# A two-layer graph network on one core: the middle part reordered, second-layer sums in three products

## The chip, the core and the metric

The kernel runs on one core of one Trainium2 chip. A core has five engines with queues of their own: TensorE (PE in the profile), VectorE (DVE), ScalarE (ACT), GpSimd (POOL) and SyncE (SP), which here issues most of the loads. They meet only through semaphores. The metric is the device time of one execution in microseconds (us), as the median over runs.

## The reference, cut to what matters

There are 625 nodes of 512 features and 10,000 edges. Layer 0 is a gated graph convolution of two steps beside a linear-attention block and a small feed-forward; layer 1 is a graph convolution with attention (`_L1_gnn_ref`) beside a second linear attention (`_L1_mix_ref`), and then two experts. The changed places are these:

```python
# layer 0, second graph step; A[r] are the 625 x 625 gated adjacencies of the two edge types
w = einsum('rb,bio->rio', att, basis)                 # 30 bases, summed per type
out = sum_r (A[r] @ (gate_r * h)) @ w[r] + h @ root + bias
# layer 1, convolution over neighbours
xb = batchnorm(xn);  agg = mean_over_neighbours(xb)   # agg = An @ xb
conv_out = relu(agg @ W_conv + b_conv)
h_attn = performer_attention(first 128 nodes) @ Wo    # later nodes repeat the last row
gnn = batchnorm(conv_out + h_attn + xn)
# layer 1, linear attention, all nodes, 8 heads of 64
q, k, v = xn @ w_qkv.T;  phi(t) = elu(t) + 1
kv = phi(k).T @ v * scale;  mix = (phi(q) @ kv) @ w_proj.T + b_proj
x = x + gnn + mix
```

## The kernel before, in words

The order of work on every engine is written out by hand: one function per engine (`block.sync`, `block.gpsimd`, `block.scalar`, `block.vector`, `block.tensor`), whose statements are that engine's queue. Nodes are handled as 5 row tiles of 125 or, with features on the partitions, as 4 feature blocks of 128 by two token halves of 312 and 313 (`HALF`). Matrices lie in eight `slot`s, whose names `row(s)` and `col(s)` say which of the two layouts is meant; `half[s]` are the same bytes under another type.

PE writes into 8 PSUM banks in a fixed rotation. `PSUM_ORDER` lists the stages and the number of tiles of each; `claim` makes PE wait until the tile eight places earlier has been read by ACT (`act_read`) or by DVE (a semaphore ending in `_out` or `_low`). So the order of stages also sets who must have finished before a bank comes free.

There are two kinds of product. A plain float32 product shows as two matmul records. The other kind splits both factors into a high and a low part of type fp32r and adds three products, high by high, high by low and low by high (`split_cols_out`, `split_rows_out`); each of these is one record. ACT, DVE or POOL makes the parts: a copy to the high part, a subtraction for the low part.

The stages in question, with the names of the code, are in order on PE:

- `o2`: `h1 @ root` (line 1456), then for both edge types r the product of the neighbour sums `Z` with the summed bases `wrel[1][r]` (line 1462), 40 plain products of 512 columns; DVE adds each row tile to x and normalises it.
- router and small feed-forward of layer 0 (lines 1472 to 1503), not touched.
- `aq`, `ak`, `av`: the three projections of the first 128 nodes. `xbr`: 20 transposes (line 1274) of the batch-normalised features to rows. `agg`: 40 plain products with the adjacency `An`, split by ACT and DVE as they come. `ad`, `uk`: squares and key features of the 128 nodes. `conv`: `agg @ W_conv`, 96 split products. `uq`, `kv`, `qfT`: the rest of the small attention's factors.
- `xqa` (half of the query projection), `at`, `atT` (line 1584), `ha` (the small attention's end), `xqb`, `xv`, `xk`, then `xkv` (phi(k).T @ v), `xo` (phi(q) @ kv), `xp` (the projection). phi is a chain of DVE (line 1134), ACT (line 755) and DVE (line 1143) per tile.
- DVE adds the convolution, `xn` and `ha` in three large steps (lines 1148 to 1152) between the first and second half of the queries, splits `xo` (line 1168), runs the second batch norm (lines 873 to 883) and adds `xp` (line 1175). `x3r`: 20 transposes back to rows, which DVE adds to x and normalises by tile (lines 1182, 861, 856); then `xeT` and the expert logits `el`.

POOL makes the split parts of the four linear weights (`split_linear`, lines 506 and 508) in two buffers that SP fills; `W_conv` is split by POOL in the same way.

## Time and profile before

| | before |
|---|---|
| median of 3 runs | 887.9 us (885.4 to 890.91) |
| the profiled execution | 887.52 us, of which 885.8 us are the span of the profile |
| mean granted TensorE clock | 0.957 |
| busy: PE, PEld, DVE, ACT, POOL | 830.7, 657.0, 527.6, 235.4, 148.8 us |
| chain that ended last | PE 87%, DVE 8%, ACT 2%, issue 2% |
| HBM read | 105.81 MB, 121 GB/s over the span |

PE is busy in 94% of the span and carries the chain. Its busy time counts records that overlap, so the length of a stage is taken here from the start of its first record to the start of the next stage. The rest of the chain (DVE, ACT, issue) is time in which PE waits for a factor that another engine prepares.

### The profile page before, as it was taken

What the parts mean: (1) busy time and instruction counts of PE and PEld (TensorE: products, weight loads), DVE (VectorE), ACT (ScalarE), POOL (GpSimd) and SP (SyncE); (2) the same over time, 40 slices, a digit from 0 to 9 for tenths busy, and PEclk for the clock granted to TensorE, in tenths of its full rate; (3) what the DMA queues carried; (4) which work ended last, traced back from release to release, by engine and by line L of the source; (5) the groups of instructions that cost most, each with busy time, mean ns of one, the idle gap of its engine ahead of it and who ended that gap; (6) DMA issues with size and microseconds to landing.
All of it is one profiled execution on the core that took longest, in us unless ns stands there. A gap on an engine that the chain in (4) does not pass through costs nothing.

```text
span 885.8 us, 10938 instructions
## 1 busy us (share of the span) xinstructions
PE 830.7 (94%) x4071; PEld 657.0 (74%) x4071; DVE 527.6 (60%) x746; ACT 235.4 (27%) x450; POOL 148.8 (17%) x96
## 2 busy tenths in 40 slices
PE   2999999998999999999998998989769999999997
PEld 1998758856667777764466698868758889998886
DVE  6877999936969999982267142946562211422112
ACT  3052223115411012220044242132342331323310
POOL 2010010021010000001000502600223431244210
PEclk9999998796999999999999998999769999999999
DMA  7732789984598768731040301000053121131101
GB/s 247 221 48 40 236 244 359 302 203 65 186 248 268 232 226 274 237 122 49 1 152 13 131 1 49 1 0 1 1 173 113 62 82 48 56 133 53 42 0 58
DMA packets 64211, 110.21 MB, mean 124 GB/s; under 512 B 6815, under 2 KB 16412, under 8 KB 64172
## 3 DMA queue, kind: packets, MB, share of 16 engines
q1 hardware_dynamic: 54476, 96.71, 32.9%
q0 software_dynamic: 6912, 7.70, 5.7%
q10 hardware_dynamic: 2784, 5.27, 1.6%
q8 instruction: 25, 0.41, 0.2%
q14 instruction: 14, 0.11, 0.0%
HBM read 105.81 MB, written 1.28 MB: 121 GB/s over the span
## 4 chain that ended last, share of the span: by engine, by line
PE 87%; DVE 8%; ACT 2%; issue 2%; DMA 1%; POOL 0%; DVEq 0%; SPq 0%; POOLq 0%
PE bank L1258 53%; PE bank L1655 13%; PE bank L1339 6%; PE bank L1462 4%; PE bank L1445 4%; PE bank L1456 2%; PE bank L1439 2%; DVE slot L1152 1%; PE bank L1267 1%; DMA slot<-in_x 1%; DVE st L861 1%; DVE slot L856 1%; ACT slot L570 1%; PE bank L1472 1%; PE bank L1274 0%
## 5 line engine op out<-in xcount | busy, mean ns | idle before, releaser
L974 DVE SCALAR_TENSOR_TENSOR weights<-weights,att 128x2048 f32<-128x2048 f32 x116 | 263.3, 2344 | 3.3 <-DMA weights<-in_L_gnn_basis 2.7
L1258 PE MATMUL bank<-half,ew_hi 128*128 128x312 f32 (+1 forms) x576 | 127.3, 310 | 2.2 <-POOL ew_lo L539 2.2
L1239 DVE CAST hid_hi<-slot 128x626 fp32r<-128x626 f32 x32 | 17.8, 557 | 159.8 <-ACT slot L817 159.8
L1258 PE MATMUL bank<-AT,slot 125*128 125x312 f32 (+1 forms) x400 | 105.9, 426 | 1.8 <-ACT slot L682 0.9
L1258 PEld LDWEIGHTS bank<-half,ew_hi 128*128 128x128 f32 x576 | 98.4, 191 | 5.9 <-issue 3.2
L1258 PEld LDWEIGHTS bank<-AT,slot 125*128 125x128 f32 x400 | 75.5, 189 | 31.8 <-ACT slot L682 1.1
L539 POOL TENSOR_TENSOR ew_lo<-weights,ew_hi 128x1024 fp32r<-128x1024 f32 x28 | 69.0, 2486 | 134.0 <-ACT ew_hi L799 134.0
L1258 PE MATMUL bank<-weights,slot 128*125 128x512 f32 (+5 forms) x306 | 90.5, 460 | 0.3 <-ACT slot L570 0.3
L1258 PE MATMUL bank<-half,ew_lo 128*128 128x312 f32 (+1 forms) x288 | 89.0, 309 | 0.0
L570 ACT ACTIVATE slot<-bank 128x312 f32<-128x312 f32 (+6 forms) x88 | 43.5, 526 | 146.9 <-PE bank L1258 107.8
L1258 PEld LDWEIGHTS bank<-weights,slot 128*125 128x125 f32 (+2 forms) x306 | 55.0, 214 | 30.2 <-issue 26.7
L817 ACT ACTIVATE slot<-bank,eb_now 128x312 f32<-128x312 f32 x64 | 33.3, 522 | 156.3 <-PE bank L1258 156.3
L1258 PE MATMUL bank<-slot,weights 128*128 128x313 f32 (+2 forms) x304 | 68.3, 386 | 0.8 <-ACT slot L570 0.8
L1258 PEld LDWEIGHTS bank<-slot,weights 128*128 128x128 f32 x304 | 51.1, 194 | 17.0 <-issue 1.5
L1655 PE MATMUL bank<-ew_lo,hid_hi 128*125 128x512 f32 x160 | 63.3, 396 | 0.0
L1655 PE MATMUL bank<-ew_hi,hid_lo 128*125 128x512 f32 x160 | 63.1, 395 | 0.0
L1655 PE MATMUL bank<-ew_hi,hid_hi 128*125 128x512 f32 x160 | 63.0, 394 | 0.0
L1339 PE MATMUL bank<-slot 125*125 125x312 f16 (+1 forms) x384 | 55.2, 306 | 1.2 <-DVE slot L959 1.1
L1339 PEld LDWEIGHTS bank<-slot 125*125 125x125 f16 x384 | 53.0, 141 | 3.1 <-DVE slot L959 1.9
L1258 PEld LDWEIGHTS bank<-half,ew_lo 128*128 128x128 f32 x288 | 55.2, 192 | 0.0
L958 DVE TENSOR_SCALAR slot<-slot,small 125x625 f16<-125x625 f16 x96 | 39.2, 408 | 13.9 <-issue 4.6
L570 ACT ACTIVATE slot<-bank,cols 128x312 f32<-128x312 f32 (+1 forms) x42 | 21.8, 526 | 87.6 <-PE bank L1445 46.4
(275 smaller groups left out, 1095.1 us busy)
## 6 DMA issues: line engine op xcount, KB each, us to landing
weights<-in_L_gnn_basis SPq DMA_DIRECT2D x60, 1024.0 KB, 5.5
weights<-in_L_ffn_W SPq DMA_DIRECT2D x32, 512.0 KB, 4.4
weights<-in_L_mix_kqv_w SPq DMA_DIRECT2D x1, 3072.0 KB, 10.3
weights<-in_w_qkvT SPq DMA_DIRECT2D x3, 1024.0 KB, 5.4
slot<-slot POOLq DMA_DIRECT2D x10, 250.0 KB, 5.2
weights<-in_L_mix_mlp_w ACTq DMA_DIRECT2D x2, 1024.0 KB, 16.4
weights<-in_L_gnn_root ACTq DMA_DIRECT2D x2, 1024.0 KB, 7.8
slot<-in_row_mlp_b POOLq DMA_DIRECT2D x1, 1250.0 KB, 34.0
```

What stands on the lines that cost most here:

```text
L539: pool.tensor_tensor(ew_lo[:, c % 4, at:at + 1024], weights[:, 2048 * (c % 2) + at:2048 * (c % 2) + at + 1024], ew_hi[:, c % 4, at:at + 10 ...
L570: act.activation(dst, src, func, **kw).then_inc(S("act_read"), 1)
L817: act.activation(hid[:, f % 4, a:a + w], B("eh", n % 3)[:, 0:w], ACT.Silu, bias=eb1_now[:, f:f + 1]).then_inc(S("eh_out"), 1)
L958: dve.tensor_scalar(oh_src[j % 2][u], iota_src, small[0:P, bass.ds(EU * q0 + EU * i + u, 1)], None, ALU.is_equal)
L974: ins = dve.scalar_tensor_tensor(wrel[layer][r], wmat(at), att[:, layer, r, b:b + 1], wrel[layer][r], ALU.mult, ALU.add)
L1239: dve.tensor_copy(hid_hi[:, f % 4, :], hid[:, f % 4, :]).then_inc(S("hid_high"), 1)
L1258: ins = pe.matmul(out, a, b, start=i == 0, stop=i == len(pairs) - 1)
L1339: ins = pe.matmul(bkq[0:P, 0:w], oh_dst[j % 2][u][:, P * r:P * r + P], oh_src[j % 2][u][:, a:a + w], start=False, stop=False)
L1439: pe.matmul(bk[:, 0:w], root[0][:, k, 128 * m:128 * m + 128], xnT[:, k, a:a + w], start=k == 0, stop=False)
L1445: ins = pe.matmul(B("h1T", n)[:, 0:w], wrel[0][r][:, k, 128 * m:128 * m + 128], col(Z_AT[r])[:, k, a:a + w], start=False, stop=i == 2 * KT ...
L1462: ins = pe.matmul(B("o2", j)[0:P, :], col(Z_AT[r])[:, k, P * j:P * j + P], wrel[1][r][:, k, :], start=False, stop=r == 1 and k == KT - 1)
L1655: ins = pe.matmul(B("eb2", j)[0:P, :], a, b, start=f == 0 and i == 0, stop=f == 15 and i == 2)
```

## The change

The function of every stage and the reference's values stay; what changes is this.

1. `o2`: the 40 plain products with `wrel[1]` become 120 split products. ACT makes the high parts (two of `Z`, two of the weights), DVE the low parts, after the last base has been summed.
2. The convolution's weight goes ahead of the neighbours: `xbw = xb @ W_conv` as 60 split products by rows, then `conv` as 40 plain products of `xbw` with `An`. The transposes `xbr` and the split of `agg` go; the split is now of `xb`, which comes with its bias from DVE's batch norm. `uk` and `ad` stand before `xbw`. POOL splits `W_conv` before the squares, and SP loads it earlier.
3. Keys and values (`xk`, `xv`) go ahead of the queries; `xkv` lies between `atT` and `ha`; `xq` is one stage of eight tiles, and `xq`, `xo` and `xp` go by token halves (`by_half`). DVE adds `xn` between the key tiles and `ha` between the query tiles, feature block by feature block.
4. `xp` and `x3r` become one stage `xpr` of 13 tiles: the first two row tiles are transposed after the fifth and the sixth tile of the projection, and DVE takes up the rows in that order.

On PE, the start of the middle part before (`weights 128x128` are `aq` and `ak`, line 1274 is `xbr`, `AT` is the adjacency, `half` the split `agg`):

```order
L1258 MATMUL bank<-slot,weights 128x128 x32
L1258 MATMUL bank<-weights,slot 128x512 x4
L1274 MATMUL bank<-ident,slot 125x128 x20
L1258 MATMUL bank<-AT,slot 128x312 x5
...
L1258 MATMUL bank<-halfsum,slot 128x2 x8
L1258 MATMUL bank<-weights,slot 128x256 x8
L1258 MATMUL bank<-half,ew_hi 128x312 x2
L1258 MATMUL bank<-half,ew_lo 128x312
...
L1258 MATMUL bank<-slot 128x65 x16
```

And the same place now (`ew_lo,half` are the split products `xbw`):

```order
L1291 MATMUL bank<-slot,weights 128x128 x32
L1291 MATMUL bank<-weights,slot 128x512 x4
L1291 MATMUL bank<-weights,slot 128x256 x8
L1291 MATMUL bank<-halfsum,slot 128x2 x8
L1291 MATMUL bank<-ew_lo,half 125x512 x60
...
L1291 MATMUL bank<-AT,slot 128x312 x5
L1291 MATMUL bank<-AT,slot 128x313 x5
...
L1291 MATMUL bank<-slot 128x65 x16
```

The 20 transposes are gone, the adjacency's products stand behind the weight's, and no 312-column split product is left in this part.

On DVE, from the first query tiles to the second batch norm, now (`bank,tmp` ends phi, lines 1188 and 1189 add `ha`, line 1197 splits `xo`):

```order
L1149 TENSOR_SCALAR tmp<-bank 128x312 [waits xq_out,psum_full]
L1188 TENSOR_TENSOR slot<-slot 128x128 [waits res,act_read]
L1189 TENSOR_SCALAR slot<-slot 128x497
L1159 SCALAR_TENSOR_TENSOR slot<-bank,tmp 128x312 [waits xexp]
L1149 TENSOR_SCALAR tmp<-bank 128x313 [waits xq_out,psum_full]
...
L1197 TENSOR_TENSOR hid_lo<-bank,hid_hi 128x312 [waits act_read,dve_step]
...
L885 BN_STATS tmp<-slot 128x6 [waits res]
```

Before, the additions were one block ahead of the last four query tiles:

```order
L1148 TENSOR_TENSOR slot<-slot 128x4x625 [waits act_read]
L1150 TENSOR_TENSOR slot<-slot 128x4x128 [waits act_read,dve_step]
L1152 TENSOR_SCALAR slot<-slot 128x497 x4
L1154 MEMSET slot 128x512 [waits dve_step]
L1134 TENSOR_SCALAR tmp<-bank 128x312 [waits xq_out,psum_full]
```

The four feature blocks are now added one at a time, each ahead of the step that ends a query tile's phi.

The diff, cut to its core:

```diff
-              ("xn2A", 12), ("aq", 1), ("ak", 1), ("av", 1), ("xbr", 5), ("agg", 8),
-              ("ad", 1), ("uk", 4), ("conv", 8), ("uq", 4), ("kv", 3), ("qfT", 4),
-              ("xqa", 4), ("at", 2), ("atT", 1), ("ha", 1),
-              ("xqb", 4), ("xv", 5), ("xk", 5), ("xkv", 1), ("xo", 8), ("xp", 8), ("x3r", 5),
+              ("xn2A", 12), ("aq", 1), ("ak", 1), ("av", 1), ("uk", 4), ("ad", 1), ("xbw", 5), ("uq", 4), ("conv", 8),
+              ("kv", 3), ("qfT", 4), ("xk", 5), ("at", 2), ("xv", 5), ("atT", 1), ("xkv", 1), ("ha", 1),
+              ("xq", 8), ("xo", 8), ("xpr", 13),
...
+def by_half(n):
+
+    return n % 4, HALF[n // 4]
...
+        z2_hi, z2_lo = (half[2], half[3]), (half[5], half[6])
+        w2_hi = [t.rearrange("p (k n) -> p k n", k=KT) for t in (ew_hi[:, 1, :], ew_lo[:, 0, :])]
+        w2_lo = [ew_hi[:, 2 + r, :].rearrange("p (k n) -> p k n", k=KT) for r in range(2)]
...
+        xb_hi, xb_lo = half[5], half[3]
+        conv_hi, conv_lo = (ew_lo[:, b, :].rearrange("p (k n) -> p k n", k=KT) for b in (1, 2))
...
+        xbw, xk_row, xv_row, xq, res = row(6), row(6), row(3), col(4), col(5)
...
+            load(W_conv, I["L1_gnn_W_conv"].rearrange("(k p) n -> p k n", p=128), "Wconv_in")
             load(Wq, I["L1_gnn_Wq"].rearrange("(k p) n -> p k n", p=128), "Wqkvo_in")
+            sp.wait_ge(S("psum_full"), filled("o2", 5))
             load(Wk, I["L1_gnn_Wk"].rearrange("(k p) n -> p k n", p=128), "Wqkvo_in")
-            sp.wait_ge(S("psum_full"), filled("o2", 5))
...
-            load(W_conv, I["L1_gnn_W_conv"].rearrange("(k p) n -> p k n", p=128), "Wconv_in")
...
+            sp.wait_ge(S("conv_split"), 1)
...
+            pool.wait_ge(S("Wconv_in"), 16)
+            pool.wait_ge(S("o2_low"), 4)
+            pool.tensor_copy(conv_hi, W_conv).then_inc(S("conv_high"), 1)
+            pool.wait_ge(S("conv_high"), 1)
+            pool.tensor_tensor(conv_lo, W_conv, conv_hi.bitcast(f32), ALU.subtract).then_inc(S("conv_split"), 1)
             pool.wait_ge(S("act_read"), READ0["ak"] + 1)
...
-            split_linear(0, filled("av", 1))
             pool.wait_ge(S("kmax"), 1)
             pool.partition_all_reduce(amax_kr, amax_k, 128, bass.bass_isa.ReduceOp.max).then_inc(S("kmax_all"), 1)
-            split_linear(1, filled("conv", 8))
-            split_linear(2, filled("ha", 1))
-            split_linear(3, filled("uq", 4))
+            pool.wait_ge(S("xb_low"), 4)
+            split_linear(0, filled("av", 1))
+            split_linear(1, filled("xbw", 5))
+            split_linear(2, filled("uq", 4))
+            split_linear(3, filled("ha", 1))
...
+                    if l == 1 and n % 8 == 7:
+                        act.wait_ge(S("act_read"), READ0["Z2"] + n + 1)
+                        act.activation(z2_hi[r][:, :, 0:N], col(Z_AT[r])[:, :, 0:N], ACT.Copy).then_inc(S("o2_high"), 1)
+            for r in range(2):
+                act.wait_ge(S("w_sum"), SUM_AT[1, NB - 1, r])
+                act.activation(w2_hi[r], wrel[1][r], ACT.Copy).then_inc(S("o2_high"), 1)
...
+            for r in range(2):
+                dve.wait_ge(S("o2_high"), r + 1)
+                dve.tensor_tensor(z2_lo[r][:, :, 0:N], col(Z_AT[r])[:, :, 0:N], z2_hi[r][:, :, 0:N].bitcast(f32),
+                                  ALU.subtract).then_inc(S("o2_low"), 1)
+                dve.wait_ge(S("o2_high"), r + 3)
+                dve.tensor_tensor(w2_lo[r], wrel[1][r], w2_hi[r].bitcast(f32), ALU.subtract).then_inc(S("o2_low"), 1)
...
+                dve.wait_ge(S("xb_high"), k + 1)
+                dve.tensor_tensor(xb_lo[:, k, 0:N], col(3)[:, k, 0:N], xb_hi[:, k, 0:N].bitcast(f32), ALU.subtract).then_inc(S("xb_low"), 1)
...
+            def add_xn2(n):
+                if n < KT:
+                    dve.wait_ge(S("act_read"), READ0["conv"] + 8)
+                    dve.tensor_tensor(res[:, n, 0:N], res[:, n, 0:N], col(2)[:, n, 0:N], ALU.add).then_inc(S("res"), 1)
+
+            phi(0, TT, add_xn2)
...
-            dve.wait_ge(S("act_read"), READ0["conv"] + 8)
-            link(dve.tensor_tensor(col(6)[:, :, 0:N], col(6)[:, :, 0:N], col(2)[:, :, 0:N], ALU.add))
-            dve.wait_ge(S("act_read"), READ0["ha"] + 1)
-            dve.tensor_tensor(col(6)[:, :, 0:NA], col(6)[:, :, 0:NA], haT, ALU.add)
-            for k in range(KT):
-                ins = dve.tensor_scalar(col(6)[:, k, NA:N], col(6)[:, k, NA:N], haT[:, k, NA - 1:NA], None, ALU.add)
-            link(ins)
...
+                if 0 <= k < KT:
+                    dve.wait_ge(S("act_read"), READ0["ha"] + 1)
+                    dve.wait_ge(S("res"), 4)
+                    dve.tensor_tensor(res[:, k, 0:NA], res[:, k, 0:NA], haT[:, k, :], ALU.add)
+                    dve.tensor_scalar(res[:, k, NA:N], res[:, k, NA:N], haT[:, k, NA - 1:NA], None, ALU.add).then_inc(S("res"), 1)
+
+            phi(TT, TT + 8, add_ha)
...
+            batchnorm(res, res, "g2", "bn2")
             dve.wait_ge(S("bn2"), 4)
...
+            def xp_tile(n):
+                m, (a, w) = by_half(n)
+                dve.wait_ge(S("psum_full"), filled("xpr", XP_TILE[n] + 1))
+                dve.scalar_tensor_tensor(res[:, m, a:a + w], B("xpr", XP_TILE[n])[:, 0:w], bsum[:, m:m + 1], res[:, m, a:a + w],
+                                         ALU.add, ALU.add).then_inc(S("xp_out"), 1)
+
             def x3_row(j):
-                dve.wait_ge(S("psum_full"), filled("x3r", j + 1))
-                dve.tensor_tensor(x[:, j, :], B("x3r", j)[0:P, :], x[:, j, :], ALU.add).then_inc(S("x3r_out"), 1)
+                for n in ((0, 1, 2, 3, 4), (5,), (6, 7), (), ())[j]:
+                    xp_tile(n)
+                dve.wait_ge(S("psum_full"), filled("xpr", X3_TILE[j] + 1))
+                dve.tensor_tensor(x[:, j, :], B("xpr", X3_TILE[j])[0:P, :], x[:, j, :], ALU.add).then_inc(S("x3r_out"), 1)
...
+            def split_cols(out, wh, wl, th, tl, m, a):
+                w = 314 if a else 312
+                return group(out[:, 0:w], [(wt[:, k, 128 * m:128 * m + 128], t[:, k, a:a + w]) for k in range(KT)
+                                           for wt, t in ((wh, th), (wh, tl), (wl, th))])
...
-                pe.wait_ge(S("w_sum"), SUM_AT[1, NB - 1, r])
+                pe.wait_ge(S("o2_low"), 2 * r + 2)
                 for j in range(TT):
                     for k in range(KT):
-                        ins = pe.matmul(B("o2", j)[0:P, :], col(Z_AT[r])[:, k, P * j:P * j + P], wrel[1][r][:, k, :],
-                                        start=False, stop=r == 1 and k == KT - 1)
+                        for i, (t, wt) in enumerate(((z2_hi, w2_hi), (z2_hi, w2_lo), (z2_lo, w2_hi))):
+                            ins = pe.matmul(B("o2", j)[0:P, :], t[r][:, k, P * j:P * j + P], wt[r][:, k, :],
+                                            start=False, stop=r == 1 and k == KT - 1 and i == 2)
                     if r == 1:
...
-            pe.wait_ge(S("xbT"), 4)
-            to_rows("xbr", col(3))
-            pe.wait_ge(S("act_read"), READ0["xbr"] + 5)
-            pe.wait_ge(S("act_read"), READ0["xn2A"] + 12)
...
+            bk = claim(pe, "ad")
...
+            pe.wait_ge(S("xb_low"), 4)
             pe.wait_ge(S("conv_split"), 1)
-            split_cols_out("conv", conv_hi, conv_lo, agg_hi, agg_lo)
+            for j in range(TT):
+                bk = claim(pe, "xbw", j)
+                group(bk[0:P, :], [(t[:, k, P * j:P * j + P], wt[:, k, :]) for k in range(KT)
+                                   for t, wt in ((xb_hi, conv_hi), (xb_hi, conv_lo), (xb_lo, conv_hi))]).then_inc(S("psum_full"), 1)
...
+            pe.wait_ge(S("act_read"), READ0["xbw"] + 5)
+            for n in range(8):
+                m, (a, w) = n // 2, HALF[n % 2]
+                bk = claim(pe, "conv", n)
+                group(bk[:, 0:w], [(xbw[:, i, 128 * m:128 * m + 128], An[:, i, a:a + w]) for i in range(TT)]).then_inc(S("psum_full"), 1)
...
-            split_cols_out("xqa", lin(ew_hi, "q"), lin(ew_lo, "q"), hid_hi, hid_lo, range(4))
+            split_rows_out("xk", "k")
...
+            pe.wait_ge(S("lin_split"), 2)
+            split_rows_out("xv", "v")
             bk = claim(pe, "atT")
...
+            bk = claim(pe, "xkv")
+            pe.wait_ge(S("xk_out"), 5)
+            pe.wait_ge(S("act_read"), READ0["xv"] + 5)
+            for p in range(KT):
+                ins = group(bk[:, 128 * p:128 * p + 128], [(xk_row[:, j, 128 * p:128 * p + 128], xv_row[:, j, 128 * p:128 * p + 128]) for j in range(TT)])
...
             pe.wait_ge(S("lin_split"), 3)
...
+            for n in range(8):
+                m, (a, w) = by_half(n)
+                split_cols(claim(pe, "xq", n), lin(ew_hi, "q"), lin(ew_lo, "q"), hid_hi, hid_lo, m, a).then_inc(S("psum_full"), 1)
...
+                m, (a, w) = by_half(n)
                 bk = claim(pe, "xo", n)
-                group(bk[:, 0:w], [(kvb[:, m, :], col(3)[:, m, a:a + w])]).then_inc(S("psum_full"), 1)
-            pe.wait_ge(S("xo_low"), 8)
+                pe.wait_ge(S("xq_out"), n + 1)
+                group(bk[:, 0:w], [(kvb[:, m, :], xq[:, m, a:a + w])]).then_inc(S("psum_full"), 1)
...
+            def projected(n):
+                m, (a, w) = by_half(n)
+                bk = claim(pe, "xpr", XP_TILE[n])
+                pe.wait_ge(S("xo_low"), 4 * (n // 4) + 4)
+                split_cols(bk, lin(ew_hi, "proj"), lin(ew_lo, "proj"), hid_hi, hid_lo, m, a).then_inc(S("psum_full"), 1)
+
+            def sum_row(j):
+                bk = claim(pe, "xpr", X3_TILE[j])
+                pe.wait_ge(S("xp_out"), 4 if j < 2 else 8)
+                for k in range(KT):
+                    ins = pe.transpose(bk[0:P, 128 * k:128 * k + 128], res[:, k, P * j:P * j + P], ident[:, :])
+                ins.then_inc(S("psum_full"), 1)
+
+            for n in range(8):
+                projected(n)
+                if n in (4, 5):
+                    sum_row(n - 4)
+            for j in range(2, TT):
+                sum_row(j)
```

## Rows read from the trace of the kernel before

**Rows 1.** Windows: length, busy time of each engine, PEclk (granted clock), DMA share, GB/s.

```profile
413.80:448.20 34.40, 34.40 (x82) 15.03 (x81) 7.45 (x16) 0.59 (x2) 0.00 (x0) 1.00 0.00 0
488.00:624.22 136.22, 126.53 (x728) 110.73 (x728) 63.34 (x101) 37.77 (x79) 36.10 (x15) 0.96 0.08 27
512.50:516.30 3.80, 3.80 (x33) 3.38 (x32) 1.35 (x3) 1.90 (x3) 0.00 (x0) 1.00 0.00 0
541.94:543.64 1.70, 1.70 (x8) 1.70 (x7) 0.00 (x0) 0.72 (x2) 1.70 (x1) 0.50 0.00 0
541.94:549.80 7.86, 7.86 (x51) 7.86 (x50) 0.00 (x0) 0.72 (x2) 2.77 (x1) 0.88 0.38 133
559.47:566.45 6.98, 6.98 (x51) 6.98 (x50) 6.95 (x3) 0.60 (x1) 6.52 (x2) 1.00 0.01 2
566.45:580.40 13.95, 13.56 (x60) 10.55 (x59) 13.09 (x12) 2.00 (x5) 8.90 (x3) 1.00 0.01 1
597.37:603.70 6.33, 6.33 (x40) 6.14 (x40) 0.00 (x0) 0.00 (x0) 0.00 (x0) 0.73 0.01 3
629.32:642.95 13.63, 11.44 (x60) 11.12 (x60) 7.72 (x18) 7.16 (x14) 6.30 (x5) 0.62 0.00 1
```

**Rows 2.** PE's timeline: start, length, instruction, [idle before it <- releaser].

```profile
477.19 7.31 PE L1258 MATMUL bank<-slot,weights 128*128 128x128 f32 x64
...
488.01 2.45 PE L1274 MATMUL bank<-ident,slot 128*125 128x128 f32 x20
...
491.35 21.30 PE L1258 MATMUL bank<-AT,slot 125*128 125x312 f32 x80 [0.90 <-ACT slot L570]
...
532.42 3.79 PE L1258 MATMUL bank<-slot 128*128 128x65 f32 x32
...
538.61 3.68 PE L1567 MATMUL bank<-ident,slot 128*128 128x128 f32 x16 [2.40 <-DVE slot L1112]
...
554.49 0.63 PE L1584 MATMUL bank<-ident,slot 128*128 128x128 f32 x4 [1.02 <-DVE slot L1119]
...
555.90 3.81 PE L1258 MATMUL bank<-slot,weights 128*128 128x128 f32 x32 [0.78 <-ACT slot L570]
...
597.37 6.33 PE L1258 MATMUL bank<-slot 125*128 125x128 f32 x40 [2.22 <-issue]
...
604.65 4.48 PE L1258 MATMUL bank<-slot 128*128 128x312 f32 x16 [0.95 <-DVE slot L1162]
...
610.17 0.41 PE L1258 MATMUL bank<-hid_hi,ew_hi 128*128 128x312 f32 x1 [1.04 <-DVE hid_lo L1168]
...
624.88 2.45 PE L1274 MATMUL bank<-ident,slot 128*125 128x128 f32 x20 [0.64 <-DVE slot L1175]
```

**Rows 3.** DVE's timeline, same columns.

```profile
393.98 0.41 DVE L1001 CAST b_split<-slot 1x512 fp32r<-1x512 f32 x1
...
524.66 2.76 DVE L1104 TENSOR_TENSOR hid_lo<-slot,hid_hi 128x2500 fp32r<-128x2500 f32 x1
...
564.10 12.00 DVE L1152 TENSOR_SCALAR slot<-slot 128x497 f32<-128x497 f32 x4
...
610.03 3.17 DVE L873 BATCH_NORM_STATS2 tmp<-slot 128x6 f32<-128x312 f32 x8
...
617.39 2.34 DVE L1175 SCALAR_TENSOR_TENSOR slot<-bank,small,slot 128x312 f32<-128x312 f32 x5
...
629.32 0.68 DVE L1182 TENSOR_TENSOR slot<-bank,slot 125x512 f32<-125x512 f32 x1
```

**Rows 4.** Line 1152 alone: nanoseconds least, median, most; first and last start.

```profile
L1152 DVE TENSOR_SCALAR slot<-slot x4: 465/3464/4841, 564.1 to 575.6; 128x497 f32<-128x497 f32 x4
```

**Rows 5.** POOL's timeline, columns as in rows 2.

```profile
396.87 5.72 POOL L487 TENSOR_TENSOR AT<-AT 125x3125 f32<-125x3125 f32 x1 [143.24 <-PE bank L1258]
...
563.71 4.94 POOL L508 TENSOR_TENSOR ew_lo<-weights,ew_hi 128x2048 fp32r<-128x2048 f32 x1
```

**Rows 6.** Groups of instructions, ACT: busy us, mean ns, idle before.

```profile
L613 ACT ACTIVATE slot<-slot 128x2500 f32<-128x2500 f32 x1 | 2.3, 2279 | 0.0
```

More of the change, by code:

```diff
@@ L735, in _ @@
                 act.activation(ke[:, h, :], ub("uk", h), ACT.Exp, bias=abias_k[:, h:h + 1]).then_inc(S("act_read"), 1)
-            for n in range(8):
-                m, (a, w) = n // 2, HALF[n % 2]
-                copy_out("conv", n, col(6)[:, m, a:a + w], B("conv", n)[:, 0:w], ACT.Relu, bias=colvec("b_conv", m))
+            for j in range(TT):
+                copy_out("xbw", j, xbw[:, j, :], B("xbw", j)[0:P, :])
             act.wait_ge(S("qbias"), 1)
@@ L867, in _, with batchnorm @@
             bns = [0]
-            def batchnorm(src, dst, gain, name):
+            def batchnorm(src, dst, gain, name, bias=None):
                 for k in range(KT):
```

187 lines of the change are left out of this document (75 added, 112 removed), and 4 rows, old and new, of the table ACT_READS.

## The prediction

> **What bounds the kernel now.** I read the page for the chain that ended last, then PE's timeline from the second layer's sums to the experts, then windows over the same stretch for the granted clock, then DVE's and POOL's timelines beside it. The order matters: the chain says that PE decides, the timeline says where PE waits, the windows say at which of its two levels (1.2 or 2.4 GHz) it works there.
>
> Three things are to be seen. First, `o2` with `wrel[1]` is 34.4 us of unbroken PE work at full clock [rows 1]. Second, from the end of `av` (488.00) to the last product of `xp` (624.22) there are 136.22 us, in which PE is busy for 126.53 [rows 1]; the waits are short and many: 0.90 before the adjacency, 2.40 before `qfT`, 1.02 and 0.78 around `atT`, 2.22 before `xkv`, 0.95 and 1.04 around `xo` [rows 2]. Third, some waits are paid twice, because the granted clock falls behind them: the first 1.70 us of `xqa`, behind the 2.40, run at 0.50, and `xkv`, behind the 2.22, at a mean of 0.73 [rows 1]. After `xp`, DVE takes the rows: its third row tile starts at 629.32 [rows 3], and from there to the last expert logit PE needs 13.63 us at 0.62 of its clock [rows 1].
>
> **The change part by part.** Prices of PE work come from [rows 1] and [rows 2].
>
> *Second-layer sums.* 40 plain products take 34.4 us. A split product of 512 columns costs 13.95/60 = 0.2325 us (`xv`, the same form, full clock [rows 1]); 120 of them take 27.9. Gain **6.5 us**, if the parts are ready. The last base is summed before 393.98 [rows 3], PE comes to the products at 413.80 and to those of the second type 14 us later. ACT copies a high part of 2500 columns in 2.28 [rows 6]; its last four pieces follow the last `Z` tile at about 397 and end by about 406 at that price. DVE's low parts cost up to 2.76 each [rows 3]. The first pair waits for the third copy, at about 402 to 404, and ends by 407; the second pair by about 412. POOL's 5.72 us addition [rows 5] lies beside them; put wholly in front of them it would move the pairs to 413 and 418, against needs of 413.8 and about 427.8. So the preparation costs nothing here; without that cover it would be up to 9.6 us. DVE's mean of the adjacency and POOL's split of `W_conv` are queued behind it, and have until the first row of `o2` and until `xbw`.
>
> *Middle part on PE.* I add up what stands between the end of `av` and the last product of `xp`, each at full clock:
> `uk` and `ad` 3.8; `xbw` 60 split products of 512 columns, 13.95; `uq` 2.1 (the same share of the 3.8 as `uk`); the adjacency's products 21.15 (491.35 to 512.50, the same shapes); `kv` 3.8; `qfT` 16 transposes at 2.45/20, 2.0; `xk` 13.95; `at` 3.7, as `kv`; `xv` 13.95; `atT` 0.5; `xkv` 40 records of 128 columns at 7.31/64, 4.5; `ha` 3.6; `xq` twice 6.98, 13.96; `xo` 4.5; `xp` 13.96; two transposed rows inside it, 1.0. Sum 120.4.
>
> New waits: `xbw` needs `xb`'s low part. ACT's four copies and DVE's four subtractions follow the batch norm, about where the bias additions ended before (488.0); PE has `uk` and `ad` to do until 491.8, so nothing. If POOL's two squares held DVE up, there are 3 us to spare. `xk` needs the split of `xn`, which DVE begins only when the convolution is out of PE, and behind which its key tiles are queued: a copy and a subtraction of 2500 columns, at most twice 2.76 [rows 3], 5.5 us; PE has `kv` and `qfT`, 5.8 us. So again nothing, but this cover is the thinnest. The key tiles come every 2.79 us (13.95/5) and DVE has three steps for each, which at 0.77 (2.34/5 for 312 columns [rows 3], by 512/312) are 2.3. `xkv` no longer waits for phi, since `xv` and `atT` lie between. The `xo` tiles need one query tile each. One wait does come: the batch norm starts on DVE about 1 us behind `xo` and takes 617.39 - 610.03 = 7.4, then four tiles of `xp` at 2.34/5, 1.9, in all 10.3; PE has five projection tiles, 8.7, before it wants the first row. **1.5 us**.
>
> Together 121.9 against 136.22: gain **14.3 us**. The queues that were passed: SP's linear weights now wait for the split of `W_conv`, long done, and `xk` needs the first of them 47 us behind `av`; POOL's splits, with 4.94 us for the longer of their two steps [rows 5], fit between.
>
> *Rows.* Before, DVE's third row started 5.1 us after the last projection product (629.32 - 624.22). Now two rows are done by then, and what is left is the last tile (0.5), one row's transposes (0.5) and two handovers: 1.3. Gain **3.8 us**. What follows up to the experts I leave as it was, 13.63 us at the low clock.
>
> The sum is 6.5 + 14.3 + 3.8 = 24.6. The profiled execution took 887.52 us, 1.7 of them outside the span, so 862.9; it stands 0.4 below the median of 887.9, so I say **863 us**.
>
> At one place a rule speaks against the change, and the row behind it is this: four DVE additions of 128x497 in one form took from 465 to 4841 ns, 12.0 us together, while POOL's weight splits ran beside them [rows 3 to 5]. I take those as three that waited for a POOL instruction each. The Trainium skill (SBUF — State Buffer, on the port pair that DVE and GpSimd share) says that this is an exclusive lock, held for a whole instruction, so the later one blocks fully; the trace agrees, 4.84 us is one 4.94 us POOL instruction. By that rule the spread-out additions could be caught as the block was.
>
> For the split products the skill (TensorE: Matmul & The Clock Gate, back-to-back issue gap) gives N/2.4 + 2.5 ns, 216 ns at 512 columns. By an estimate from that page `o2` would gain 8.5 and the total would be 861; the trace's 232 ns decides, and I keep 6.5.
>
> **The rivals.**
>
> *POOL catches the additions.* Here the four blocks of `ha` are added between query tiles, and POOL's fourth split starts when `ha` is out of PE, at the same moment as the queries. DVE's own work in the query stage is, at 0.47 a step of 312 columns, 16 steps of phi and 4 x 0.67 for the additions, 10.2 of 13.9 us. Three blocked additions as before add 12.0 - 4 x 0.465 = 10.1, and one of the shorter ones perhaps 1.7: 22 us, 8 beyond the stage, and `xo` waits for it. 863 + 8 = **871 us**. For: the row. Against: POOL's two steps take at most 2 x 4.94, likelier under 7 (a copy reads one factor, the subtraction two), and the first addition comes with the fourth query tile, 7 us after `ha`.
>
> *The clock stays up behind `xp`.* PE's 11.44 busy us of the tail at 0.62 would be 7.1 at full clock, 4.3 less; DVE's rows would pace it then, so I take 3: **860 us**. For: two rows are ready and there is less idle time. Against: the work is the same few columns.
>
> *The parts of `o2` come late or the split form gains nothing there*: 6.5 us stay away, **869 us**.
>
> *Slower: the clock.* The rows at 0.50 show the split product of 312 columns at about 0.26 us instead of 0.145, a factor of 1.8 [rows 1]. `ad`, products of two columns, now stands directly before 60 split products. If PE fell to the lower level there and stayed, the five split stages, 69.8 us, would cost 56 us more: 863 + 56 = **919 us**. It decides against the change once about 31 us more of PE work run at the lower level than before. Against it: `ad` and `uk` ran at 1.00 [rows 1], and behind a pause the clock was back after 1.7 us.
>
> **How the numbers follow.** Forecast (860.5 to 867) 0.60; caught additions 0.14; the higher clock behind `xp` 0.11; `o2` without gain 0.06; slower by the clock 0.03; unnamed new waits in the reordered middle that eat most of the gain, 879 and above, 0.06. The range 857 to 872 holds all but the last two and a little at the edges, about 0.85. About 1% is what a measurement of this kernel can tell from no change. Faster by over 1% is below 879: 0.92. Within 1%: 0.05. Slower by over 1%: 0.03.
>
> **What would show it right or wrong.** `o2` at 27.9 us and no wait before it. `av` to the end of `xp` at about 122 us, with one wait of some 1.5 us, before the first row's transposes, and all of it at a clock near 1.00, `qfT` at 2.0 and `xkv` at 4.5. The third row on DVE 1.3 us behind the last projection product. The additions of `ha` at 0.47 us each. A gap before `xbw` or before `xk` of over 1 us, a clock below 0.9 in the middle, or an addition of several us would each make a term wrong; a gain of under 15 us in total makes the theory of waits wrong.

## The result and the profile after

The changed kernel takes **864.16 us** (median of 4 runs, 862.23 to 864.79) against 887.7 of the kernel before (885.4 to 890.91): a ratio of 0.9731, with a 95% interval of 0.9709 to 0.9754. The forecast was 863 us, with 857 to 872 as its range, so it held. The profiled execution took 864.79 us with a span of 863.0, so 22.8 us less than the span of 885.8; the steps of the sum had 24.6.

I cut both profiles at the same events on PE and compare the pieces. The cuts of the kernel after, as windows (start and end, length, PE busy with its count, granted clock, DMA share, GB/s): `o2`'s split products; from there to the end of `av`; two pieces inside that; the middle part to the last product of `xp`; the rows up to the last expert logit; and, inside the middle, `qfT` and `xkv`.

```profile
core 0: us, PE busy (x), PEclk, DMA share, GB/s
412.68:440.94 28.26, 28.26 (x122) 1.00 0.00 1
440.94:484.03 43.09, 39.03 (x226) 0.92 0.29 94
445.44:450.50 5.06, 5.06 (x33) 0.66 1.05 394
469.29:473.24 3.95, 3.95 (x22) 0.57 0.00 0
484.03:605.71 121.68, 119.61 (x680) 1.00 0.09 30
605.71:620.55 14.84, 11.62 (x72) 0.74 0.00 1
...
562.63:567.17 4.54, 4.54 (x41) 1.00 0.00 0
528.55:530.40 1.85, 1.85 (x19) 1.00 0.00 0
```

| Piece | before | after | difference | the sum had |
|---|---|---|---|---|
| start to `o2`'s relation products | 413.78 | 412.68 | -1.1 | 0 |
| these products | 34.34 | 28.26 | -6.1 | -6.5 |
| transposes, router, feed-forward, `aq` to `av` | 39.88 | 43.09 | **+3.2** | 0 |
| end of `av` to last product of `xp` | 136.24 | 121.68 | -14.6 | -14.3 |
| from there to DVE's third row | 5.08 | 1.43 | -3.7 | -3.8 |
| third row to last expert logit | 13.64 | 13.41 | -0.2 | 0 |
| experts to the end | 242.84 | 242.45 | -0.4 | 0 |
| span | 885.8 | 863.0 | -22.8 | -24.6 |

The three terms of the sum gave 24.3 us. What is missing of the 24.6 stands above all in the third line, which the change does not touch (+3.2, against -1.7 in the lines that the sum had at nothing): the two windows at 0.66 and 0.57 are a router stage and a piece of transposes that ran at half clock here and at full clock before.

PE's timeline of the kernel after shows the waits that are left in the middle (start, duration, line, operation, and in brackets the idle time before it and what ended it). The last row is the first one behind `xp`.

```profile
528.55 1.92 PE L1599 MATMUL bank<-ident,slot 128*128 128x128 f32 x16
...
562.63 4.70 PE L1291 MATMUL bank<-slot 125*128 125x128 f32 x40 [0.34 <-ACT slot L581]
...
599.37 0.67 PE L1653 MATMUL bank<-ident,slot 128*125 128x128 f32 x4 [1.73 <-DVE slot L1208]
...
606.43 1.55 PE L1653 MATMUL bank<-ident,slot 128*125 128x128 f32 x12 [0.73 <-DVE slot L1208]
```

`qfT` has no wait and takes 1.92 us instead of 3.68 [rows 2]; `xkv` has 0.34 us of wait instead of 2.22, and 4.70 instead of 6.33. One wait of 1.73 us stands before the first summed row. The seven waits of [rows 2] that the prediction lists have become these two. An eighth was there, 0.39 us at 578.16 inside `xv`, which rows 2 leave out; all idle time of PE in this part came to 9.7 us before (136.22 - 126.53) and comes to 2.1 now (121.68 - 119.61).

DVE's timeline has the preparation of `o2`'s low parts:

```profile
400.69 3.83 DVE L1030 TENSOR_TENSOR ew_hi<-weights,ew_hi 128x2048 fp32r<-128x2048 f32 x1 [3.89 <-ACT ew_hi L704]
404.45 2.75 DVE L1027 TENSOR_TENSOR half<-slot,half 128x2500 fp32r<-128x2500 f32 x1
407.12 2.28 DVE L1030 TENSOR_TENSOR ew_hi<-weights,ew_lo 128x2048 fp32r<-128x2048 f32 x1
409.32 3.39 DVE L1033 TENSOR_REDUCE small<-AT 125x5 f32<-125x3125 f32 x1
412.75 3.35 DVE L1034 TENSOR_SCALAR small<-small 125x5 f32<-125x5 f32 x1
```

The first pair is there at 404.5 and the second at 409.4; PE comes to them at 412.68 and 14 us later. The first of these steps took 3.83 us where its twin took 2.28: POOL's addition on the adjacency (L498) ran until 402.38 beside it. And this is the third row on DVE (first line), 1.4 us behind `xp`, and the last normalised row:

```profile
607.14 0.69 DVE L1215 TENSOR_TENSOR slot<-bank,slot 125x512 f32<-125x512 f32 x1 [0.86 <-PE bank L1653]
...
613.86 1.29 DVE L868 TENSOR_SCALAR slot<-slot,mv,rs 125x512 f32<-125x512 f32 x1
...
620.59 0.20 DVE L1223 TENSOR_TENSOR slot<-bank,small 125x40 f32<-125x40 f32 x1 [5.44 <-PE bank L1291]
```

From the last normalised row (615.2) DVE waits 5.4 us for logits that PE makes at half clock.

### The profile page after: what moved, and what is told of

Same layout as the page of the kernel before. It is cut to its first block, busy times and chain, and to the rows that moved or that the text cites. A ratio compares the mean times of both kernels' runs of the same rounds, so it can differ in the third digit from the quotient of the medians.

```text
span 863.0 us, 10928 instructions
## 1 busy us (share of the span) xinstructions
PE 816.1 (95%) x4055; PEld 656.4 (76%) x4055; DVE 535.3 (62%) x752; ACT 240.8 (28%) x446; POOL 148.5 (17%) x96
## 4 chain that ended last, share of the span: by engine, by line
PE 90%; DVE 6%; issue 1%; ACT 1%; DMA 1%; POOL 0%; DVEq 0%; SPq 0%; POOLq 0%
PE bank L1291 56%; PE bank L1703 13%; PE bank L1370 6%; PE bank L1476 4%; PE bank L1493 3%; PE bank L1487 2%; PE bank L1470 2%; PE bank L1300 1%; DMA slot<-in_x 1%; DVE st L873 1%; PE bank L1503 1%; DVE slot L868 1%; PE bank L1307 1%; DVE slot L1096 0%; DVE tmp L885 0%
## 5 line engine op out<-in xcount | busy, mean ns | idle before, releaser
L1291 PE MATMUL bank<-half,ew_hi 128*128 128x314 f32 (+1 forms) x512 | 113.0, 310 | 2.1 <-POOL ew_lo L550 2.1
L1272 DVE CAST hid_hi<-slot 128x626 fp32r<-128x626 f32 x32 | 15.8, 493 | 159.4 <-ACT slot L829 159.4
L1291 PEld LDWEIGHTS bank<-half,ew_hi 128*128 128x128 f32 x512 | 87.6, 191 | 5.6 <-issue 2.9
L1291 PE MATMUL bank<-weights,slot 128*125 128x512 f32 (+5 forms) x306 | 87.3, 450 | 0.3 <-ACT slot L581 0.3
L1291 PE MATMUL bank<-half,ew_lo 128*128 128x312 f32 (+1 forms) x256 | 79.0, 309 | 0.0
L1291 PEld LDWEIGHTS bank<-half,ew_lo 128*128 128x128 f32 x256 | 49.0, 191 | 0.0
```

Source lines behind the costliest of these rows:

```text
L1291: ins = pe.matmul(out, a, b, start=i == 0, stop=i == len(pairs) - 1)
```

## The experiments

Eleven kernels and a second run of the changed one. Ratios are to the kernel before on the same chip; the changed kernel has 0.9731 (0.9709 to 0.9754).

### The second-layer sums: one part undone, one part alone

`e1_plain_o2` undoes the product form in the changed kernel:

```diff
-for i, (t, wt) in enumerate(((z2_hi, w2_hi), (z2_hi, w2_lo), (z2_lo, w2_hi))):
-    ins = pe.matmul(B("o2", j)[0:P, :], t[r][:, k, ...], wt[r][:, k, :], ...)
+ins = pe.matmul(B("o2", j)[0:P, :], z2_hi[r][:, k, ...].bitcast(f32), w2_hi[r][:, k, :].bitcast(f32), ...)
```

> The changed kernel, with o2's products as 40 plain ones on the high parts alone (the low parts are still made, and left out of the sum). Theory, o2 pays by the form of its products: the stage takes 34.3 us again instead of 28.3, so the kernel is 6.1 us slower than the changed one, 870.3 us. If the two stretches at half clock behind o2 (3.2 us, after the sums and before aq) come from o2 having become shorter, they go away too, and the total is 867. Rival, the gain of the change comes from the middle alone: 864.2 as before the edit.

`e2_only_o2` puts ACT's four copies, DVE's four subtractions and PE's products of the change into the kernel before, and nothing else:

```diff
 for r in range(2):
-    pe.wait_ge(S("w_sum"), SUM_AT[1, NB - 1, r])
+    pe.wait_ge(S("o2_low"), 2 * r + 2)
...
-ins = pe.matmul(B("o2", j)[0:P, :], col(Z_AT[r])[:, k, ...], wrel[1][r][:, k, :], ...)
+for i, (t, wt) in enumerate(((z2_hi, w2_hi), (z2_hi, w2_lo), (z2_lo, w2_hi))):
+    ins = pe.matmul(B("o2", j)[0:P, :], t[r][:, k, ...], wt[r][:, k, :], ...)
```

> The kernel before, with the split products of o2 and their preparation alone. Theory: o2 from 34.3 to 28.3 us and no wait before it, 887.7 - 6.1 = 881.6 us; with the two half-clock stretches behind it, if they belong to the shorter o2, 884.8. Rival, the preparation delays something: 887.7 or more.

Measured: 869.24 us (0.9798, 0.9768 to 0.9828) and 881.91 us (0.9942, 0.9919 to 0.9965). The windows of PE for the stage and for what follows up to `aq`, first of `e1_plain_o2`:

```profile
414.82:449.15 34.33, 34.33 (x81) 1.00 0.00 0
449.15:478.23 29.08, 25.02 (x153) 1.00 0.35 116
```

and of `e2_only_o2`:

```profile
414.75:443.00 28.25, 28.25 (x123) 1.00 0.00 1
443.00:472.07 29.07, 25.01 (x153) 1.00 0.34 117
```

The form of the products is worth 6.1 us wherever it stands, and the medians say 5 to 6. The stretch behind it took 29.07 us with the short `o2` and 29.08 with the long one, so the half-clock pieces do not come from `o2` being shorter.

### The rows: behind the projections, and one tile later

`e3_rows_last` has the rows where they were, `e4_row_one_later` moves the first two by one tile (the tables of tiles go with it, and in `e3_rows_last` DVE's order):

```diff
 for n in range(8):
     projected(n)
-    if n in (4, 5):
-        sum_row(n - 4)
-for j in range(2, TT):
+for j in range(TT):            # e3_rows_last
     sum_row(j)
...
-    if n in (4, 5):
-        sum_row(n - 4)
+    if n in (5, 6):            # e4_row_one_later
+        sum_row(n - 5)
```

> The changed kernel, with all five summed rows behind the eighth projection tile as in the kernel before. Theory as in the prediction: DVE's third row starts 5.1 us behind the last projection product instead of 1.5, and the 1.7 us wait and 1.2 us of transposes inside the projections go: 3.6 - 1.7 - 1.2 = 0.7 us slower, 864.9. Rival, the rows inside the projections are worth the 3.8 us that the prediction gave them as a term: 867.8. Second rival, the wait made in front of the first row eats it all: 864.2 or less.

> The changed kernel, with the first two summed rows each one projection tile later (behind the sixth and the seventh). Theory: the wait of 1.7 us before the first row is covered by one more tile of 1.75 us, and DVE's rows come no later: 864.2 - 1.7 = 862.5. Rival, DVE paces the rows from the batch norm on, and the saved wait turns up again before the third row: 864.2.

Measured: 866.79 us (0.9781, 0.9749 to 0.9813) and 863.08 us (0.9732, 0.9695 to 0.9768). Windows of PE in `e3_rows_last`, from the last product of `xp` to DVE's third row and on to the last logit:

```profile
600.13:605.26 5.13, 2.42 (x20) 1.00 0.00 0
605.26:619.14 13.88, 12.13 (x60) 0.52 0.00 1
```

The handover takes the old 5.1 us, and the projections end 2.8 us sooner since neither wait nor transposes stand among them. From `aq` to the third row the kernel needs 134.77 us (470.49 to 605.26) against 133.90 (473.24 to 607.14), 0.9 more, and to the last logit 1.3 more. So the place of the rows is worth about 1 us by the profile, not its 3.8 alone. The median is 2.6 us higher, and by the ratios it would be 4.4; the intervals just overlap, and I leave open how much of that is real.

In `e4_row_one_later` the wait before the first row is gone, but half of it is back before the third:

```profile
598.68 0.67 PE L1653 MATMUL bank<-ident,slot 128*125 128x128 f32 x4
600.93 0.60 PE L1653 MATMUL bank<-ident,slot 128*125 128x128 f32 x4
604.88 1.55 PE L1653 MATMUL bank<-ident,slot 128*125 128x128 f32 x12 [1.60 <-DVE slot L1208]
```

That wait was 0.73 us in the changed kernel. From `aq` to the last logit the gain is 0.9 us (146.41 against 147.31), too little for the medians. DVE, not PE, paces the rows here.

### POOL's split against DVE's additions

```diff
-split_linear(3, filled("ha", 1))
+split_linear(3, filled("xq", 4))
```

> The changed kernel, with POOL's fourth weight split started by the fourth query tile (about 577.5) instead of by ha (571.0), so that it meets DVE's additions of ha. Theory of the prediction's first rival: a DVE addition that meets POOL's 4.6 us subtraction waits for it; the split lies at 577.5 to 584, the additions at 578.3 to 584.2; one or two DVE steps are stretched by up to 1.9 and 4.6 us, DVE has about 3 us to spare in what is left of the stage, so xo comes about 3.5 us late: 867.7. Rival: the two engines run beside each other, all additions at 0.47 and 0.28 us: 864.2.

Measured: 868.15 us (0.9798, 0.9775 to 0.9822). POOL's two steps in `e7_split_late`:

```profile
575.81 1.90 POOL L516 CAST ew_hi<-weights 128x2048 fp32r<-128x2048 f32 x1 [58.89 <-PE bank L1291]
577.79 4.61 POOL L518 TENSOR_TENSOR ew_lo<-weights,ew_hi 128x2048 fp32r<-128x2048 f32 x1
```

and DVE beside them:

```profile
575.72 0.48 DVE L1149 TENSOR_SCALAR tmp<-bank 128x312 f32<-128x312 f32 x1 [0.86 <-PE bank L1291]
576.11 1.74 DVE L1188 TENSOR_TENSOR slot<-slot 128x128 f32<-128x128 f32 x1
577.78 4.90 DVE L1189 TENSOR_SCALAR slot<-slot 128x497 f32<-128x497 f32 x1
582.60 0.47 DVE L1159 SCALAR_TENSOR_TENSOR slot<-bank,tmp 128x312 f32<-128x312 f32 x1
...
583.57 0.28 DVE L1188 TENSOR_TENSOR slot<-slot 128x128 f32<-128x128 f32 x1
583.77 0.47 DVE L1189 TENSOR_SCALAR slot<-slot 128x497 f32<-128x497 f32 x1
```

One addition ends with POOL's cast, the next with its subtraction; the same forms take 0.28 and 0.47 when POOL is idle. From `aq` to the last product of `xp` it costs 4.85 us (137.32 against 132.47). In the changed kernel POOL's subtraction ran from 573.01 to 577.62 and the first addition began at 578.26: the rival of the prediction was missed by 0.6 us:

```profile
573.01 4.61 POOL L518 TENSOR_TENSOR ew_lo<-weights,ew_hi 128x2048 fp32r<-128x2048 f32 x1
576.54 0.47 DVE L1159 SCALAR_TENSOR_TENSOR slot<-bank,tmp 128x312 f32<-128x312 f32 x1
578.26 0.28 DVE L1188 TENSOR_TENSOR slot<-slot 128x128 f32<-128x128 f32 x1
```

### The old block of additions left out of the kernel before

`e9_before_no_ha` leaves out the addition of `ha` to the residual:

```diff
 dve.wait_ge(S("act_read"), READ0["ha"] + 1)
-dve.tensor_tensor(col(6)[:, :, 0:NA], col(6)[:, :, 0:NA], haT, ALU.add)
-for k in range(KT):
-    ins = dve.tensor_scalar(col(6)[:, k, NA:N], col(6)[:, k, NA:N], haT[:, k, NA - 1:NA], None, ALU.add)
```

> The kernel before, with the addition of ha to the residual left out (five DVE instructions, 12 us of blocked additions in its profile). Theory of the prediction: that block stands beside xv's 14 us on PE, and nothing waits for DVE there before xkv, so leaving it out is worth nothing: 887.7, or 0.6 less at most. Rival: the block made DVE late for the key tiles and so for xkv's 2.2 us wait, and its removal in the changed kernel was part of the gain: 887.7 - 2.2 - 1.8 (xkv at full clock) = 883.7.

Measured: 888.42 us (0.9998, 0.9977 to 1.0019). The largest stall in DVE's timeline of the kernel before was worth nothing that the runs can tell. One thing waited for it, and briefly: PE, in `xv`, for a bank that DVE read only behind the additions. First that wait, in the kernel before; it is gone in `e9_before_no_ha`. Then the wait before `xkv` in the latter, the same as in [rows 2], but without the slow `xkv` behind it; and the same in `e2_only_o2`, whose order is also that of the kernel before:

```profile
578.16 0.49 PE L1258 MATMUL bank<-ew_hi,hid_hi 128*125 128x512 f32 x1 [0.39 <-DVE slot L1143]
...
604.96 4.70 PE L1254 MATMUL bank<-slot 125*128 125x128 f32 x40 [2.22 <-issue]
...
592.18 4.70 PE L1275 MATMUL bank<-slot 125*128 125x128 f32 x40 [2.22 <-issue]
```

### The order of keys and values, and of the queries' features

`e8_values_first` has `xv`, `at`, `xk`, `atT`, `xkv` on PE, and DVE's attention block ahead of its key tiles:

```diff
-split_rows_out("xk", "k")
+pe.wait_ge(S("lin_split"), 2)
+split_rows_out("xv", "v")
 ...                            # at
-pe.wait_ge(S("lin_split"), 2)
-split_rows_out("xv", "v")
+split_rows_out("xk", "k")
```

> The changed kernel, with xv ahead of xk again (at between them), as in the kernel before. Theory: xkv waits for the last key tile's three steps on DVE and ACT, 2.2 us as before, instead of 0.34, and PE's clock falls behind it so that xkv's 40 products take 6.3 instead of 4.7 us: 864.2 + 1.9 + 1.6 = 867.7. Rival 1: only the wait, the clock stays: 866.1. Rival 2: atT's transposes and the two attention blocks cover it, 864.2.

`e10_uq_behind_conv` has the queries' random features behind the neighbour products on PE, and ACT's exponentials behind its copies of `conv`:

```diff
-random_features("uq", aqT)
 for n in range(8):
     ...                        # the neighbour products, stage "conv"
+random_features("uq", aqT)
```

> The changed kernel, with the queries' random features uq and what follows them on ACT and DVE behind the neighbour products again, as in the kernel before. Theory: the maxima, the exponentials (3.0 us) and DVE's last step take 6.3 us behind uq, PE has only kv's 3.7 before qfT, so it waits about 2.6 there (2.40 in the kernel before); DVE begins the split of xn2 only then, 4.5 us against qfT's 2, so a second wait of about 2.5 stands before xk. Both are followed by work at half clock: qfT 3.7 instead of 1.9 us, and up to 2 us more in xk. 864.2 + 5.1 + 1.8 + 2.0 = 873.1. Rival 1, the waits without the clock: 869.3. Rival 2, the features' place does not matter because kv and other work cover it: 864.2.

Measured: 867.8 us (0.9795, 0.9772 to 0.9818) and 873.19 us (0.9831, 0.9799 to 0.9863). Windows of `e8_values_first`, the pause before `xkv` and the stage (with the start of `ha`):

```profile
558.19:560.49 2.30, 0.00 (x0) 1.00 0.00 0
560.49:566.80 6.31, 6.31 (x42) 0.73 0.00 0
```

and PE's timeline of `e10_uq_behind_conv`:

```profile
534.10 3.67 PE L1599 MATMUL bank<-ident,slot 128*128 128x128 f32 x16 [4.04 <-DVE slot L1128]
538.55 0.79 PE L1291 MATMUL bank<-ew_hi,hid_hi 128*125 128x512 f32 x1 [0.78 <-DVE hid_lo L1133]
```

Keys first is worth 3.6 us from `aq` to the end of `xp` (136.02 against 132.47): 2.0 of wait, 1.6 of clock. In `e10_uq_behind_conv` the two waits are 4.04 and 0.78 where 2.6 and 2.5 were expected. Their sum is 4.8 instead of 5.1: DVE's last step on the queries takes 2.56 us, not the 1.3 I reckoned, and PE runs the transposes at half clock (1.8 us more), which covers most of the split of `xn`. A window over the 4.45 us from 538.55 on shows the clock at 0.50 in `xk` too. From `aq` to the end of `xp` it is 10.2 us more (142.71 against 132.47): 5.5 of waits, with 0.69 that appears before the neighbour products, 1.8 in `qfT`, 2.5 in `xk` (16.31 us up to `at`, against 13.83), the rest in small pieces. So the total came out as forecast (873.19 against 873.1), but not by the waits that I had expected.

### Extra products in PE's pauses

`e5_fill_middle` and `e6_fill_tail` give PE work of no use while it would wait; the results are overwritten. Shown is the place of `e5_fill_middle` and of the first 14 products of `e6_fill_tail`; 26 more stand ahead of PE's waits in the routing (`en`, `combT`, `eh`). That makes 40, where the expectations below say 41:

```diff
+def fill(bk, n):
+    for _ in range(n):
+        pe.matmul(bk[:, 0:128], ident[:, :], ident[:, :], start=True, stop=True)
 def tile_to_cols(stage, n, j, src, ready):
     bk = claim(pe, stage, n)
+    fill(bk, FILL.get((stage, j), 0))
     pe.wait_ge(S(ready), j + 1)
```

> The changed kernel, with 10 extra products of 128 columns (0.23 us each, results overwritten) put in front of three of PE's waits between o2 and aq (behind o2's rows 2 before xfT's fourth tile; 4 each before the third and fourth xn2 tile). In the profile of the changed kernel this stretch had two pieces at half clock (0.66 and 0.57 in their windows) and took 32.3 us; in the kernel before and in three of four experiments so far it took 29.1. Theory: short pauses let the clock go at times; with PE busy in them the stretch takes 29.1 us at 1.00, and the total is 864.2 less 0 to 3.2, so about 862.7. Rival: the pauses are not what lowers the clock, the two pieces stay and the total is 864.2. Second rival, the extra products delay the transposes behind them: up to 10 x 0.23 = 2.3 us more, 866.5.

> The changed kernel, with 41 extra products of 128 columns (results overwritten) in PE's waits between the third summed row and the first expert product: 14 around the transposes of the last layer norm, 27 while DVE routes. Theory: PE's stretch before the routing ran at 0.58 and 0.50 and the first expert products at half clock because PE paused; kept busy it stays at 1.00. The last logit then comes about 2.4 us after the last normalised row instead of 5.4 (3.0 us less), and the first four groups of expert products take 0.52 instead of 0.78 us (1.0 us less, and 0.6 for the first two of the next): 864.2 - 4.6 = 859.6. Rival: DVE's rows and POOL's split of the expert weights pace this stretch whatever the clock: 864.2, with the clock at 1.00. Second rival: short products don't hold the clock, 864.2 with the clock at 0.5.

Measured: 863.23 us (0.9733, 0.9709 to 0.9757) and 860.13 us (0.9704, 0.9681 to 0.9726).

In `e5_fill_middle` the stretch from `o2` to `aq` took 28.96 us at a clock of 1.00. That proves little, for the stretch differs between executions of one program. The changed kernel, run again (`after_again`), shows it whole, at 29.08:

```profile
444.38:473.46 29.08, 25.02 (x152) 1.00 0.36 116
473.46:484.26 10.80, 10.80 (x76) 1.00 0.21 59
484.26:605.92 121.66, 119.59 (x680) 1.00 0.09 30
605.92:621.00 15.08, 12.43 (x72) 0.69 0.00 1
```

> The changed kernel itself, as the measure for the one above on the same chip, and a second profile of the stretch between o2 and aq: 864.2. If the two half-clock pieces there belong to this program, the stretch takes 32.3 us again; if they differ from execution to execution, any of 29.1, 30.7 or 32.3.

It measured 866.24 us (0.9733, 0.9705 to 0.9762). So the 3.2 us belong to one execution, not to the change. Over the profiles of this study this stretch, with its pauses of 0.73 and twice 1.18 us, ran whole at full clock in six without extra products, had one piece at half clock (30.7 us) in four, two such pieces in the profile after, and a longer one at its head in `e9_before_no_ha`. With extra products it was whole in both profiles taken. By chance alone that would happen about one time in four, so for this place the theory is supported and not shown.

At the end of the kernel it is shown, since there every profile without extra products has the slow piece. Windows of `e6_fill_tail`, from the last product of `xp` to the last logit, then the routing, then the first expert products:

```profile
605.18:617.85 12.67, 11.79 (x101) 1.00 0.01 1
617.85:625.55 7.70, 6.42 (x41) 0.78 0.41 135
630.10:636.00 5.90, 5.90 (x41) 1.00 0.43 129
```

and of the changed kernel the last of these (the first, 14.84 us at 0.74, stands in the section on the result):

```profile
633.26:637.03 3.77, 3.77 (x15) 0.55 0.08 17
```

The last logit comes 2.2 us sooner, the routing with POOL's split takes 12.25 instead of 12.71 us, and the experts to the end 228.2 instead of 229.7: 4.2 us together. The ratios say 0.27% of 887.7, 2.4 us, with intervals that overlap. That the clock is held is shown; how much time this gains is between these two figures. The routing window still has a stretch below full clock; with the same products there it ran at 1.00 in the next kernel, so this too differs from execution to execution.

### The edits together

> The changed kernel with three edits together: the extra products in PE's waits of both places (10 between o2 and aq, 41 from the summed rows to the experts), and the first two summed rows one projection tile later. Theory: the gains add. Behind the last logit 4.2 us as measured in the profile of the kernel with the later extra products alone, 0.9 from the rows, and 0 to 3.2 between o2 and aq: 864.2 - 5.1 - 1.0 = 858. Rival: with the clock held, DVE paces the rows either way and the later rows bring nothing more: 859.5.

`b1_all` takes **857.66 us** (5 runs, 857.18 to 858.63; ratio 0.9655, 0.9629 to 0.9681), against 866.24 us of the changed kernel on the same chip. It beats both kernels: by 0.8% the changed one by the ratios (0.9655 to 0.9733, and the intervals are apart), by 3.5% the one before. Its windows, `o2` to `aq`, `xp` to the last logit, and from there to the first expert product:

```profile
441.67:470.62 28.95, 27.38 (x172) 1.00 0.35 118
601.34:614.88 13.54, 11.78 (x102) 1.00 0.01 1
614.88:626.98 12.10, 8.46 (x65) 1.00 0.53 175
```

From `aq` to the end of the span it needs 384.8 us (855.4 - 470.62), the changed kernel 389.8, and the one with the later extra products alone 385.6: the later rows bring 0.8 on top, not nothing.

## Why the prediction was right

*Second-layer sums, -6.5.* Right: 28.26 us, 6.1 less than before, with no wait. The mean is 28.26/120 = 0.2355 us a product instead of 0.2325, which is the missing 0.4; it stands in the first 60 products (412.68 to 427.01, 14.33 us), while the second 60 took 13.93, 0.232 each. The price itself came from a window that does not fit its stage: `xv` went on until 581.08, not 580.40, and held the wait of 0.39; the two errors nearly cancel (`xk` behind it, without a wait, took 14.07 us, 0.2345 a product). The preparation cost nothing, as the two pairs were ready 8 and 17 us before PE wanted them. One part alone and one part undone gave the same 6.1. The formula in the Trainium skill (TensorE: Matmul & The Clock Gate, back-to-back issue gap) would give 216 ns a product and, as an estimate, 8.5 us of gain; the trace does not agree, with 235.5 ns, and the trace decides.

*Middle part, -14.3.* Right in size (-14.6) and by its parts: `uk` and `ad` 3.7, `xbw` 14.1, `uq` 2.0, the neighbours 21.1, `kv` 3.5, `qfT` 1.9, `xk` 13.8, `xv` 13.9, `xkv` 4.5 at full clock. The only wait of size was the predicted one, 1.73 instead of 1.5 us, and 0.34 before `xkv`, which I had at nothing. Two small errors cancel in the total: PE's work came to 119.6 us where the sum had 120.4, the waits to 2.1 where it had 1.5. Set side by side, the two profiles divide the 14.6 so: 7.6 us of waits; 4.3 of half clock (`qfT` 1.8, the head of `xqa` 0.9, `xkv` 1.6); 2.4 of transposes that are gone; less 1.3 for the two rows that came in; the rest of about 1.5 in small pieces. The runs confirm the mechanism at two places: keys ahead of values is worth 3.6 us, the queries' features ahead of the neighbours 10.2. The second is not a share of the 14.6, since `e10_uq_behind_conv` also makes the split of `xn` late, which the kernel before did earlier. No run undoes the convolution's order (item 2 of the change) by itself; its share is read from the profiles alone.

*Waits paid twice.* That a wait is followed by work at half clock (the lower of the two levels, 0.50 in the windows) carried 1.8 us of `qfT` and 1.8 of `xkv` in the sum. `e8_values_first` and `e10_uq_behind_conv` brought both back (6.3 and 3.67 us). But it does not always happen: behind the same 2.22 us `xkv` took 4.70 us in `e9_before_no_ha` and in `e2_only_o2`. Of three profiles with the old order only one has the slow `xkv`, the one that the prediction was made from; in the other two there was nothing to give back at this place. Against `e2_only_o2`, whose middle part took 134.55 us (482.88 to 617.43), the reordering is worth 12.9 us, not 14.6: part of the hit is luck in which execution was profiled.

*Rows, -3.8.* The handover fell from 5.08 to 1.43 us. As a term it is right only together with the 1.5 and 1.0 us that the same move put into the middle. Net the prediction had 1.3 us, and undoing the move cost 0.9 by the profile up to the third row and 1.3 up to the last logit.

*Nothing elsewhere.* Here the sum was off, by 3.2 us the wrong way in the stretch before `aq`. The second profile of the same program shows it at 29.08 us, so the profile after, at 863.0, caught it in the longer of the two forms seen in this kernel. A further 1.7 us fell the other way, of which 1.1 before `o2`, which also differs from execution to execution (412.7 to 416.1 in two profiles of the changed kernel). That 864.2 came so close to 863 is therefore in part luck: these two stretches vary by more than 3 us each by themselves, and here one fell long and the other short.

*The rivals.* Caught additions (871 us): did not happen, but by 0.6 us; made to happen, they cost 4.9 us of the 8 I had given them, since one subtraction and one cast were met, not three. The higher clock behind `xp` (860): did not happen by itself (0.74, then 0.54 from 612 on); made to happen, it gave 860.1 us, with 2.2 us from the rival's own stretch, where it had 3, and the rest from the routing and the experts. `o2` without gain and the slow clock from `ad` on: refuted, 28.26 us and 1.00.

## What to carry over

Add up the work on the bounding engine at full clock and then each wait that is left, with the name of what ends it: that sum held within 0.3 us over 120 us of reordered work, with errors of 0.8 and 0.6 us that cancelled. A stall on another engine, even of 12 us, is worth no more than the wait that it causes, here 0.39 us; one on that engine with only 0.6 us of distance can be the next trap. And where the bounding engine pauses often and briefly, read the granted clock behind the pauses: work of no use put into them paid 2 to 4 us at the end of this kernel.
